# Score matmuls: the pass with the low queries on 64 of the 128 partitions, in pairs of row tiles

## The chip, the core and the metric

The program runs on one core of one Trainium2 chip. The metric is the device time of one execution in microseconds. Before the change the median of three runs is 1233.47 us (1231.24 to 1234.61).

Engines by their short names: PE (TensorE, matmuls), PEld (its weight loads), DVE (VectorE), ACT (ScalarE), POOL (GpSimd), SP (SyncE, which issues the DMAs).

## What is computed

One layer with three parts, all in float32:

```
x = x + cross_attention(layernorm(x), ctx, ctx)     # 8 batches, 64 queries, 1601 keys, 16 heads of 32
x = x + self_attention(layernorm(x)) @ Wo           # its value width is 0, so it adds nothing
x = x + moe(layernorm(x))                           # 8 experts, top 2, hidden 2048

# cross attention, the part that matters here
k = ctx @ Wk + bk ;  v = ctx @ Wv + bv              # ctx: 8 x 1601 x 384, Wk and Wv: 384 x 512
out = softmax(q @ k.T * 32**-0.5) @ v
```

## The kernel before

**Precision.** PE's single-pass float32 type (fp32r) keeps fewer bits than float32. So each operand is split into a high part (ACT or POOL rounds it) and a low part (what is left, by DVE or POOL), and a product is the sum of high times high, high times low and low times high (`three_pass`, L399).

**Attention.** The work is a sequence of 64 steps: 8 batches, and in each of them 8 steps s = 0 to 7. One step does two heads of one batch: the heads' 2 x 64 queries are the 128 columns of the weights (`qbd_hi`, `qbd_lo`; zero where a query meets the other head's rows), the two heads' 2 x 32 key dimensions are 64 rows. The 1601 keys lie in four chunks of 384, 384, 384 and 449 (computed as 450) keys; chunk c of a step has PSUM bank c for its scores.

`k_mix` holds for each step the high keys on one half of the 128 partitions and the low keys on the other half. Even steps have the high keys on partitions 0 to 63, odd steps on 64 to 127. A matmul with all 128 partitions so sums high and low keys in one pass. The queries stand on both halves. The scores of a chunk are two such matmuls: `qbd_hi` (L1321), and `qbd_lo` (L1322), which computes low queries times high keys, and low times low beside it.

**One step on PE** (`step`, L1311): the four chunks' scores; `context` of the step before (13 matmuls, L1285: probabilities times values); three units of the current projection job (`run_job`; a key unit is nine matmuls of 384 or 450 columns, a value unit nine of 256); 13 transposes of the probabilities (L1337), which write into the same four banks as the scores; the rest of the job's units. A job has five units, two of them keys, and every fourth job (that of steps 3 and 7) six. Step 0 has four small matmuls more (`spread`, L1293).

**One step on the others.** DVE takes the maximum of each chunk's scores (L955), the negated maximum of all (L958), takes up the context (L901, L911), splits off the low parts of the job's units (keys L877, values L884), then of the transposed probabilities chunk by chunk (`pt_mix`, L969), and then of the job's last two (or three) value units. ACT does the exponentials (L684, L687) after L958, then the high parts of the same units (keys L644, values L649) and of `pt_mix` (L695).

**What orders them.** Each engine runs its list in order, with semaphores between them. Three matter here: `pt_split` (DVE, one per chunk) says that a chunk's bank and the step's probabilities are read; the scores of chunk c of the next step wait for it (L1318). `scores_ready` (PE, one per chunk) releases DVE's maximum of that chunk (L954). `proj_split` gives a projection bank back.

**Setup.** The key weights are split once into `wk_hi` and `wk_lo` (L660, L859), [128, 3, 512] each. A key unit takes 128 columns of them as weights, so its PSUM rows 0 to 63 belong to the even step of a pair and rows 64 to 127 to the odd one. In the last batch the steps 4 to 7 have no projection job.

Of the kernel before, what the change touches and what calls it, by code (L numbers as in the profile page):

```python
# [25 lines left out]
ALU = mybir.AluOpType  # L26
ACT = mybir.ActivationFunctionType
# [11 lines left out]
def bass_perceiver_layer_kernel(nc, x, ctx_t, wq, bq_t, wk, bk_t, wv, bv_t, wo, bo, router_w, router_b,  # L39
# [54 lines left out]
    with ExitStack() as stack:  # L94
        def sb(name, shape, dt, where=stack):
            return where.enter_context(nc.sbuf_tensor(name, shape, dt))
# [10 lines left out]
        bq_sb = sb("bq_sb", [P, KD], F32)  # L107
        bk_sb = sb("bk_sb", [P, KD], F32)
        bv_sb = sb("bv_sb", [P, KD], F32)
# [55 lines left out]
        ctx_lo = [place(f"ctx_lo{i}", [P, KC, KEYS_PAD], F32R, attn) for i in range(2)]  # L165
        wk_hi = place("wk_hi", [P, KC, D], F32R, attn)
        wk_lo = place("wk_lo", [P, KC, D], F32R, attn)
        wv_hi = place("wv_hi", [P, KC, D], F32R, attn)
        wv_lo = place("wv_lo", [P, KC, D], F32R, attn)
        attn.close()  # L170

# [198 lines left out]
        def first_queries(quad, copy):  # L370
# [4 lines left out]
                    slice(NQ * (quad % 2), NQ * (quad % 2 + 1)))  # L375

        def x1_bank(t):

            return PROJ_BANK + t if t < TILES_BEFORE else t - TILES_BEFORE
# [29 lines left out]
        def _(sp):  # L409
# [16 lines left out]
            sp.dma_start(bq_sb[:], bq_t).then_inc(bias_loaded, 16)  # L426
            sp.dma_start(bk_sb[:], bk_t).then_inc(bias_loaded, 16)
            sp.dma_start(bv_sb[:], bv_t).then_inc(bias_loaded, 16)
# [191 lines left out]
        def _(act):  # L620
# [15 lines left out]
            def proj_high_part(unit, n, bank):  # L636

                kind, a, c = unit
                act.wait_ge(proj_ready, n + 1)
                if kind == "keys":  # L640
                    m = KEYS_EVEN[c]
                    for i in range(2):
                        rows = slice(i * HALF, (i + 1) * HALF)
                        last = nc.scalar.activation(k_mix[rows, 2 * a + i, KEY0[c]:KEY0[c] + m], ps[rows, bank, 0:m],  # L644
                                                    ACT.Identity, bias=bk_sb[rows, a:a + 1])
# [13 lines left out]
            act.wait_ge(wkv_loaded, 32)  # L659
            nc.scalar.copy(wk_hi[:], wkv_raw[:, 0]).then_inc(wkv_high, 1)  # L660
            nc.scalar.copy(wv_hi[:], wkv_raw[:, 1]).then_inc(wkv_high, 1)
            act.wait_ge(bias_loaded, 48)
            for c in range(CHUNKS):
# [156 lines left out]
        def _(dve):  # L820
# [36 lines left out]
            for i, (hi, lo) in enumerate([(wk_hi, wk_lo), (wv_hi, wv_lo)]):  # L857
                dve.wait_ge(wkv_high, i + 1)
                nc.vector.tensor_tensor(lo[:], wkv_raw[:, i], hi[:].bitcast(F32), ALU.subtract).then_inc(wkv_split, 1)  # L859
            dve.wait_ge(bias_loaded, 48)  # L860
            for m in range(KD):
# [7 lines left out]
            def proj_low_part(unit, n, bank):  # L869
                kind, a, c = unit  # L870
                dve.wait_ge(proj_high, n + 1)
                if kind == "keys":
                    m = KEYS_EVEN[c]
                    cols = slice(KEY0[c], KEY0[c] + m)
                    for i in range(2):
                        rows, other = slice(i * HALF, (i + 1) * HALF), slice((1 - i) * HALF, (2 - i) * HALF)
                        last = nc.vector.scalar_tensor_tensor(out=k_mix[other, 2 * a + i, cols], in0=ps[rows, bank, 0:m],  # L877
                                                              scalar=bk_sb[rows, a:a + 1],
                                                              in1=k_mix[rows, 2 * a + i, cols].bitcast(F32),
                                                              op0=ALU.add, op1=ALU.subtract)  # L880
# [342 lines left out]
        def _(pe):  # L1223
# [21 lines left out]
            def project(unit, n, bank):  # L1245
                kind, a, c = unit
                for k in range(KC):
                    if kind == "keys":
                        slot, m, cols = c % 2, KEYS_EVEN[c], slice(a * P, (a + 1) * P)
                        last = three_pass(pe, ps[:, bank, 0:m], wk_hi[:, k, cols], wk_lo[:, k, cols],  # L1250
                                          ctx_hi[slot][:, k, 0:m], ctx_lo[slot][:, k, 0:m], k == 0, k == KC - 1)
# [59 lines left out]
            def step(b, s, before, last_batch=False):  # L1311
# [4 lines left out]
                for c in range(CHUNKS):  # L1316
                    if before is not None:
                        pe.wait_ge(pt_split, CHUNKS * (n - 1) + c + 1)  # L1318
                    m = KEYS_EVEN[c]
                    cols = slice(KEY0[c], KEY0[c] + m)  # L1320
                    pe.matmul(ps[:, SCORE_BANK + c, 0:m], qbd_hi[:, s, :], k_mix[:, s, cols], start=True, stop=False)  # L1321
                    pe.matmul(ps[:, SCORE_BANK + c, 0:m], qbd_lo[:, s, :], k_mix[:, s, cols], start=False,  # L1322
                              stop=True).then_inc(scores_ready, 1)
                if before is not None:
# [228 lines left out]
```

## Time and profile before

| | us |
|---|---|
| median of 3 runs | 1233.47 |
| the profiled execution | 1227.9 |
| its span, first to last instruction | 1226.1 |
| PE busy | 1143.8 (93%) |
| DVE busy | 958.2 (78%) |
| ACT busy | 704.6 (57%) |
| POOL busy | 428.0 (35%) |

The attention steps fill some 60 to 790 us of the span; in 60 to 735 us PE is busy for 674.18 of 675.00 us at a granted clock of 1.00, DVE for 579.89 us. A busy PE means that some matmul is in flight: matmuls are pipelined, and how fast they follow one another is read from their starts, not from this share. The rest is the output projection, the router and the experts.

### The profile page before, as it was taken

How to read it: one execution, taken by the hardware profiler on the slowest of the kernel's cores; microseconds unless marked ns; L12 is line 12 of the kernel's file. 1: busy time of each engine (PE TensorE's matmuls, PEld its weight loads, DVE VectorE, ACT ScalarE, POOL GpSimd, SP SyncE). 2: the span in 40 equal slices, each digit the busy share in tenths (PEclk: the TensorE clock that was granted, in tenths of full speed). 3: DMA queues.
4: the chain of work that ended last, by engine and by line, in shares of the span. 5: the costliest groups of instructions: out<-in, count | busy, mean ns of one | idle time of the engine just before them, and what ended most of it. 6: DMA issues, size and time to landing. Idle time of an engine off the chain costs nothing.

```text
span 1226.1 us, 23151 instructions
## 1 busy us (share of the span) xinstructions
PE 1143.8 (93%) x7488; PEld 1054.2 (86%) x7489; DVE 958.2 (78%) x2082; ACT 704.6 (57%) x1418; POOL 428.0 (35%) x378
## 2 busy tenths in 40 slices
PE   4899999999999999999999998757889999889998
PEld 4799999999999999999999997635668898668897
DVE  6578888888888888888888888865876756876655
ACT  3456656656656656656656656443575565665654
POOL 5454754754654654654664640010000000000000
PEclk9899999999999999999999999966899999989999
DMA  5322122122122122122122103113755634655633
GB/s 181 101 63 62 40 70 61 38 70 61 38 70 61 38 70 61 38 70 61 39 69 61 58 23 118 50 52 105 244 189 184 206 109 164 221 191 193 201 117 103
DMA packets 74304, 121.15 MB, mean 99 GB/s; under 512 B 10776, under 2 KB 35480, under 8 KB 74272
## 3 DMA queue, kind: packets, MB, share of 16 engines
q1 hardware_dynamic: 74272, 120.73, 30.6%
q8 instruction: 19, 0.31, 0.1%
q14 instruction: 13, 0.11, 0.0%
HBM read 118.62 MB, written 2.10 MB: 98 GB/s over the span
## 4 chain that ended last, share of the span: by engine, by line
PE 79%; DVE 9%; ACT 5%; DMA 3%; issue 3%; DVEq 0%; SPq 0%; ACTq 0%
PE ps L401 18%; PE ps L403 17%; PE ps L402 17%; PE ps L1285 7%; PE ps L1337 7%; PE ps L1321 4%; PE ps L1322 3%; DMA w_raw<-in_w_dram 2%; PE ps L1386 2%; DVE w_lo L1027 2%; DVE mx L955 1%; DVE k_mix L877 1%; PE ps L1429 1%; DVE w_lo L1019 1%; PE ps L1430 1%
## 5 line engine op out<-in xcount | busy, mean ns | idle before, releaser
L545 POOL TENSOR_TENSOR ctx_hi<-ctx_raw,no_query 128x1152 fp32r<-128x1152 f32 x64 | 142.8, 2231 | 290.2 <-PE ps L403 281.2
L877 DVE SCALAR_TENSOR_TENSOR k_mix<-ps,bk_sb,k_mix 64x384 fp32r<-64x384 f32 (+1 forms) x256 | 162.3, 634 | 82.1 <-ACT k_mix L644 77.8
L684 ACT ACTIVATE probs<-ps,negmax 128x1152 f32<-128x1152 f32 x64 | 78.3, 1223 | 201.1 <-DVE negmax L958 201.1
L401 PE MATMUL ps<-wv_hi,ctx_hi 128*128 128x256 f32 (+1 forms) x624 | 181.8, 291 | 6.7 <-DVE k_mix L877 6.5
L549 POOL TENSOR_TENSOR ctx_lo<-ctx_raw,ctx_hi 128x1152 fp32r<-128x1152 f32 x64 | 179.7, 2808 | 5.0
L403 PE MATMUL ps<-wv_hi,ctx_lo 128*128 128x256 f32 (+1 forms) x624 | 175.7, 282 | 0.0
L402 PE MATMUL ps<-wv_lo,ctx_hi 128*128 128x256 f32 (+1 forms) x624 | 174.9, 280 | 0.0
L644 ACT ACTIVATE k_mix<-ps,bk_sb 64x384 fp32r<-64x384 f32 (+1 forms) x256 | 150.8, 589 | 24.0 <-PE ps L403 19.4
L969 DVE TENSOR_TENSOR pt_mix<-ps,pt_mix 128x384 fp32r<-128x384 f32 (+1 forms) x256 | 142.2, 580 | 1.4 <-ACT pt_mix L695 1.4
L401 PE MATMUL ps<-ctx_hi,wk_hi 128*128 128x384 f32 (+1 forms) x384 | 133.2, 347 | 0.0
L403 PE MATMUL ps<-ctx_hi,wk_lo 128*128 128x384 f32 (+1 forms) x384 | 132.3, 345 | 0.0
L402 PE MATMUL ps<-ctx_lo,wk_hi 128*128 128x384 f32 (+1 forms) x384 | 131.9, 344 | 0.0
L955 DVE TENSOR_REDUCE mx<-ps 128x1 f32<-128x384 f32 (+1 forms) x256 | 128.6, 564 | 0.6 <-issue 0.2
L649 ACT CAST v_mix<-ps 128x256 fp32r<-128x256 f32 (+1 forms) x208 | 77.5, 373 | 85.3 <-PE ps L403 83.4
L401 PEld LDWEIGHTS ps<-wv_hi,ctx_hi 128*128 128x128 f32 (+1 forms) x624 | 115.8, 186 | 9.1 <-DVE k_mix L877 8.1
L402 PEld LDWEIGHTS ps<-wv_lo,ctx_hi 128*128 128x128 f32 (+1 forms) x624 | 116.3, 186 | 0.3
L403 PEld LDWEIGHTS ps<-wv_hi,ctx_lo 128*128 128x128 f32 (+1 forms) x624 | 115.7, 185 | 0.0
L695 ACT CAST pt_mix<-ps 128x384 fp32r<-128x384 f32 (+1 forms) x256 | 111.5, 532 | 0.1
L1285 PEld LDWEIGHTS ps<-pt_mix,v_mix 128*128 128x128 f32 (+1 forms) x832 | 106.2, 188 | 2.1
L1285 PE MATMUL ps<-pt_mix,v_mix 128*128 128x256 f32 (+1 forms) x832 | 107.6, 279 | 0.0
L1337 PE MATMUL ps<-ident,probs 128*128 128x128 f32 (+1 forms) x832 | 101.4, 273 | 6.5 <-ACT probs L684 6.5
L401 PE MATMUL ps<-w_hi,h_hi 128*128 128x512 f32 x192 | 81.3, 423 | 19.6 <-DVE h_lo L1205 19.5
(219 smaller groups left out, 2668.5 us busy)
## 6 DMA issues: line engine op xcount, KB each, us to landing
w_raw<-in_w_dram SPq DMA_DIRECT2D x68, 1024.0 KB, 5.3
ctx_raw<-in_ctx_t_dram SPq DMA_DIRECT2D x48, 576.0 KB, 3.8
ctx_raw<-in_ctx_t_dram SPq DMA_DIRECT2D x16, 673.5 KB, 4.1
q_both<-q_scratch SPq DMA_DIRECT2D x14, 128.0 KB, 3.1
x<-in_x_dram SPq DMA_DIRECT2D x1, 1024.0 KB, 5.4
wq_raw<-in_wq_dram SPq DMA_DIRECT2D x1, 1024.0 KB, 7.7
q_scratch<-q_out SPq DMA_DIRECT2D x1, 1024.0 KB, 5.4
wo_raw<-in_wo_dram SPq DMA_DIRECT2D x1, 1024.0 KB, 5.4
```

The costliest lines, as they stand in the source:

```text
L401: pe.matmul(acc_ap, a_hi, b_hi, start=start, stop=False)
L402: pe.matmul(acc_ap, a_hi, b_lo, start=False, stop=False)
L403: return pe.matmul(acc_ap, a_lo, b_hi, start=False, stop=stop)
L545: nc.gpsimd.tensor_tensor(ctx_hi[slot][:, :, 0:n], ctx_raw[slot][:, :, 0:n], no_query[:].rearrange("p (o i) -> p o i", o=1).broadcast_to([ ...
L549: nc.gpsimd.tensor_tensor(ctx_lo[slot][:, :, 0:n], ctx_raw[slot][:, :, 0:n], ctx_hi[slot][:, :, 0:n].bitcast(F32), ALU.subtract).then_inc( ...
L644: last = nc.scalar.activation(k_mix[rows, 2 * a + i, KEY0[c]:KEY0[c] + m], ps[rows, bank, 0:m], ACT.Identity, bias=bk_sb[rows, a:a + 1])
L695: nc.scalar.copy(pt_mix[:, TILE0[c]:TILE0[c] + n, 0, :], ps[:, SCORE_BANK + c, 0:n * P].rearrange("p (t r) -> p t r", t=n)).then_inc(pt_hi ...
L877: last = nc.vector.scalar_tensor_tensor(out=k_mix[other, 2 * a + i, cols], in0=ps[rows, bank, 0:m], scalar=bk_sb[rows, a:a + 1], in1=k_mix ...
L955: part = nc.vector.tensor_reduce(mx[:, c:c + 1], ps[:, SCORE_BANK + c, 0:KEYS[c]], AX.X, ALU.max)
L969: nc.vector.tensor_tensor(pt_mix[:, TILE0[c]:TILE0[c] + m, 1, :], ps[:, SCORE_BANK + c, 0:m * P].rearrange("p (t r) -> p t r", t=m), pt_mi ...
L1285: last = pe.matmul(ps[:, PV_BANK, 0:2 * P], v_mix[0:r, t, s, :, :], pt_mix[0:r, t, :, :], start=(t == 0), stop=(t == KT - 1))
L1337: last = pe.transpose(ps[0:r, SCORE_BANK + c, i * P:(i + 1) * P], probs[:, key:key + r], ident[:])
```

## The change

The pass with `qbd_lo` takes only the 64 partitions that hold the high keys. For two chunks in a row to lie on different halves, the half with the high keys now also changes with the chunk: partitions 64 * ((s + c) % 2) and the 63 behind it. So the matmuls of chunks 0, 1, 2, 3 lie alternately in one and the other half of PE's rows. For this the projection of the odd chunks must give its two halves swapped: `wk_hi` and `wk_lo` become [128, 3, 4, 192], with the first 64 columns of each group once more at its end, an odd chunk takes columns 64 to 191, and there is a second, swapped key bias. The step issues the four `qbd_hi` matmuls first, then the four `qbd_lo` ones.

```
-                    pe.matmul(ps[:, SCORE_BANK + c, 0:m], qbd_hi[:, s, :], k_mix[:, s, cols], start=True, stop=False)
-                    pe.matmul(ps[:, SCORE_BANK + c, 0:m], qbd_lo[:, s, :], k_mix[:, s, cols], start=False,
-                              stop=True).then_inc(scores_ready, 1)
+                    pe.matmul(ps[:, SCORE_BANK + c, 0:m], qbd_hi[:, s, :], k_mix[:, s, KEY0[c]:KEY0[c] + m],
+                              start=True, stop=False)
+                for c in range(CHUNKS):
+                    m, rows = KEYS_EVEN[c], high_half(s, c)
+                    pe.matmul(ps[:, SCORE_BANK + c, 0:m], qbd_lo[rows, s, :], k_mix[rows, s, KEY0[c]:KEY0[c] + m],
+                              start=False, stop=True).then_inc(scores_ready, 1)
...
+        def high_half(s, c):
+            return slice((s + c) % 2 * HALF, ((s + c) % 2 + 1) * HALF)
...
-                        slot, m, cols = c % 2, KEYS_EVEN[c], slice(a * P, (a + 1) * P)
+                        slot, m, cols = c % 2, KEYS_EVEN[c], slice(c % 2 * HALF, c % 2 * HALF + P)
...
-            nc.scalar.copy(wk_hi[:], wkv_raw[:, 0]).then_inc(wkv_high, 1)
+            for cols, to in key_columns():
+                last = nc.scalar.copy(wk_hi[:, :, :, to], wkv_raw[:, 0].rearrange("p k (g c) -> p k g c", c=P)[:, :, :, cols])
+            last.then_inc(wkv_high, 1)
...
-            sp.dma_start(bk_sb[:], bk_t).then_inc(bias_loaded, 16)
+            sp.dma_start(bk_sb[0][:], bk_t).then_inc(bias_loaded, 16)
+            for i in range(2):
+                sp.dma_start(bk_sb[1][i * HALF:(i + 1) * HALF], bk_t[(1 - i) * HALF:(2 - i) * HALF]).then_inc(bias_loaded, 16)
```

On ACT and DVE the splits of the keys take the rows by `high_half` and the bias by the chunk's parity; their number and shapes stay. DVE's `wk_lo` is made in two pieces like `wk_hi`.

PE's list at the scores of a step and the start of the context behind them, before (k_mix are the keys, qbd_hi and qbd_lo the queries):

```order
L1321 MATMUL ps<-k_mix,qbd_hi 128x384 [waits pt_split]
L1322 MATMUL ps<-k_mix,qbd_lo 128x384
L1318 REGISTER_ALU
L1321 MATMUL ps<-k_mix,qbd_hi 128x450 [waits pt_split]
L1322 MATMUL ps<-k_mix,qbd_lo 128x450
L1280 ISA
L1281 ISA [waits proj_split]
L1282 ISA [waits pt_split]
L1285 MATMUL ps<-pt_mix,v_mix 128x256 [waits pv_free]
```

(The first three rows stand there three times.) The same place in the changed kernel:

```order
L1339 MATMUL ps<-k_mix,qbd_hi 128x384 [waits pt_split]
L1337 REGISTER_ALU
L1339 MATMUL ps<-k_mix,qbd_hi 128x450 [waits pt_split]
L1343 MATMUL ps<-k_mix,qbd_lo 128x384 x3
L1343 MATMUL ps<-k_mix,qbd_lo 128x450
L1299 ISA
L1300 ISA [waits proj_split]
L1301 ISA [waits pt_split]
L1304 MATMUL ps<-pt_mix,v_mix 128x256 [waits pv_free]
```

All four qbd_lo matmuls, and with them the first of the four releases of DVE's maxima, have moved behind the last of the four waits for `pt_split`.

DVE's list in the setup, before, from the split of the key weights to the first query tile:

```order
L855 TENSOR_TENSOR xt_lo<-ps,xt_hi 128x512 [waits xt_high] x4
L859 TENSOR_TENSOR wk_lo<-wkv_raw,wk_hi 128x1536 [waits wkv_high]
L859 TENSOR_TENSOR wv_lo<-wkv_raw,wv_hi 128x1536 [waits wkv_high]
L863 TENSOR_SCALAR q_out<-ps,bq_sb 128x512 [waits q_ready,bias_loaded]
L863 TENSOR_SCALAR q_out<-ps,bq_sb 128x512 [waits q_ready] x3
```

And in the changed kernel:

```order
L870 TENSOR_TENSOR xt_lo<-ps,xt_hi 128x512 [waits xt_high] x4
L874 TENSOR_TENSOR wk_lo<-wkv_raw,wk_hi 128x12x128 [waits wkv_high]
L874 TENSOR_TENSOR wk_lo<-wkv_raw,wk_hi 128x12x64
L878 TENSOR_TENSOR wv_lo<-wkv_raw,wv_hi 128x1536 [waits wkv_high]
L882 TENSOR_SCALAR q_out<-ps,bq_sb 128x512 [waits q_ready,bias_loaded]
L882 TENSOR_SCALAR q_out<-ps,bq_sb 128x512 [waits q_ready] x3
```

One piece of 12 x 64 elements has come in ahead of the value weights.

## Rows read from the trace of the kernel before

**Rows 1.** The page: busy time by engine; the chain that ended last, by engine.

```profile
PE 1143.8 (93%) x7488; PEld 1054.2 (86%) x7489; DVE 958.2 (78%) x2082; ACT 704.6 (57%) x1418; POOL 428.0 (35%) x378
...
PE 79%; DVE 9%; ACT 5%; DMA 3%; issue 3%; DVEq 0%; SPq 0%; ACTq 0%
```

**Rows 2.** Waits: engine, line waited for; us in total, times, longest.

```profile
DVE k_mix L877 <- ACT k_mix L644: 77.8, 73, 3.1
...
PEld ps L1321 <- DVE pt_mix L969: 12.6, 49, 0.3
```

**Rows 3.** Timeline of PE, step 6's scores: start, us, instruction, count.

```profile
317.60 0.47 PE L1321 MATMUL ps<-k_mix,qbd_hi 128*128 128x450 f32 x1
317.91 0.37 PE L1322 MATMUL ps<-k_mix,qbd_lo 128*128 128x450 f32 x1
318.11 1.64 PE L1285 MATMUL ps<-pt_mix,v_mix 128*128 128x256 f32 x13
```

**Rows 4.** Timeline of DVE, steps 5 and 6; in brackets idle time and releaser.

```profile
307.07 2.01 DVE L955 TENSOR_REDUCE mx<-ps 128x1 f32<-128x384 f32 x4
...
312.32 2.53 DVE L877 SCALAR_TENSOR_TENSOR k_mix<-ps,bk_sb,k_mix 64x384 fp32r<-64x384 f32 x4 [1.20 <-ACT k_mix L644]
...
316.39 1.15 DVE L969 TENSOR_TENSOR pt_mix<-ps,pt_mix 128x384 fp32r<-128x384 f32 x2
...
318.12 2.01 DVE L955 TENSOR_REDUCE mx<-ps 128x1 f32<-128x384 f32 x4
```

**Rows 5.** Timeline of PE, steps 0 and 1, first scores and first context.

```profile
340.08 0.34 PE L1321 MATMUL ps<-k_mix,qbd_hi 128*128 128x384 f32 x1
340.26 0.34 PE L1322 MATMUL ps<-k_mix,qbd_lo 128*128 128x384 f32 x1
...
341.55 1.69 PE L1285 MATMUL ps<-pt_mix,v_mix 128*128 128x256 f32 x13
...
352.43 0.34 PE L1321 MATMUL ps<-k_mix,qbd_hi 128*128 128x384 f32 x1
```

**Rows 6.** Timeline of DVE, steps 0 and 1, and step 0 a batch later.

```profile
341.02 2.00 DVE L955 TENSOR_REDUCE mx<-ps 128x1 f32<-128x384 f32 x4
...
353.04 0.42 DVE L884 TENSOR_TENSOR v_mix<-ps,v_mix 128x256 fp32r<-128x256 f32 x1 [0.39 <-ACT v_mix L649]
353.55 2.02 DVE L955 TENSOR_REDUCE mx<-ps 128x1 f32<-128x384 f32 x4
...
432.57 2.00 DVE L955 TENSOR_REDUCE mx<-ps 128x1 f32<-128x384 f32 x4
```

**Rows 7.** Timeline of PE, transposes and L1297's 16-row tiles, then L401.

```profile
303.17 0.60 PE L1337 MATMUL ps<-ident,probs 128*128 128x128 f32 x4
303.52 0.36 PE L401 MATMUL ps<-wv_hi,ctx_hi 128*128 128x256 f32 x1
303.72 0.28 PE L402 MATMUL ps<-wv_lo,ctx_hi 128*128 128x256 f32 x1
...
349.19 1.10 PE L1297 MATMUL ps<-rinv_t,pick 16*128 16x64 f32 x8
350.22 0.39 PE L401 MATMUL ps<-wv_hi,ctx_hi 128*128 128x256 f32 x1
350.44 0.28 PE L402 MATMUL ps<-wv_lo,ctx_hi 128*128 128x256 f32 x1
```

**Rows 8.** L1297's matmuls, by line: ns min/median/max, first and last start, forms.

```profile
L1297 PE MATMUL ps<-rinv_t,pick x64: 270/270/319, 166.0 to 794.3; 16*128 16x64 f32 x64
```

**Rows 9.** Timeline of DVE in the setup.

```profile
19.43 3.09 DVE L859 TENSOR_TENSOR wk_lo<-wkv_raw,wk_hi 128x1536 fp32r<-128x1536 f32 x1 [0.57 <-ACT wk_hi L660]
...
26.03 2.20 DVE L863 TENSOR_SCALAR q_out<-ps,bq_sb 128x512 f32<-128x512 f32 x3
30.19 0.75 DVE L863 TENSOR_SCALAR q_out<-ps,bq_sb 128x512 f32<-128x512 f32 x1 [1.97 <-PE ps L403]
```

**Rows 10.** Timeline of ACT, step 7 of the last batch.

```profile
784.68 1.22 ACT L684 ACTIVATE probs<-ps,negmax 128x1152 f32<-128x1152 f32 x1 [6.11 <-DVE negmax L958]
```

More of the change, by code:

```diff
@@ L107, in bass_perceiver_layer_kernel @@
         bq_sb = sb("bq_sb", [P, KD], F32)
-        bk_sb = sb("bk_sb", [P, KD], F32)
+        bk_sb = [sb(f"bk_sb{i}", [P, KD], F32) for i in range(2)]
         bv_sb = sb("bv_sb", [P, KD], F32)
@@ L165, in bass_perceiver_layer_kernel @@
         ctx_lo = [place(f"ctx_lo{i}", [P, KC, KEYS_PAD], F32R, attn) for i in range(2)]
-        wk_hi = place("wk_hi", [P, KC, D], F32R, attn)
-        wk_lo = place("wk_lo", [P, KC, D], F32R, attn)
         wv_hi = place("wv_hi", [P, KC, D], F32R, attn)
         wv_lo = place("wv_lo", [P, KC, D], F32R, attn)
+        wk_hi = place("wk_hi", [P, KC, GROUPS, P + HALF], F32R, attn)
+        wk_lo = place("wk_lo", [P, KC, GROUPS, P + HALF], F32R, attn)
         attn.close()
@@ L375, in first_queries, with key_columns @@
                     slice(NQ * (quad % 2), NQ * (quad % 2 + 1)))
+        def key_columns():
+            return [(slice(0, P), slice(0, P)), (slice(0, HALF), slice(P, P + HALF))]
+        def high_half(s, c):
+            return slice((s + c) % 2 * HALF, ((s + c) % 2 + 1) * HALF)
         def x1_bank(t):
@@ L642, in proj_high_part @@
                     for i in range(2):
-                        rows = slice(i * HALF, (i + 1) * HALF)
+                        rows = high_half(2 * a + i, c)
                         last = nc.scalar.activation(k_mix[rows, 2 * a + i, KEY0[c]:KEY0[c] + m], ps[rows, bank, 0:m],
-                                                    ACT.Identity, bias=bk_sb[rows, a:a + 1])
+                                                    ACT.Identity, bias=bk_sb[c % 2][rows, a:a + 1])
                     last.then_inc(proj_high, 1)
@@ L659, in _ @@
             act.wait_ge(wkv_loaded, 32)
-            nc.scalar.copy(wk_hi[:], wkv_raw[:, 0]).then_inc(wkv_high, 1)
+            for cols, to in key_columns():
+                last = nc.scalar.copy(wk_hi[:, :, :, to], wkv_raw[:, 0].rearrange("p k (g c) -> p k g c", c=P)[:, :, :, cols])
+            last.then_inc(wkv_high, 1)
             nc.scalar.copy(wv_hi[:], wkv_raw[:, 1]).then_inc(wkv_high, 1)
-            act.wait_ge(bias_loaded, 48)
+            act.wait_ge(bias_loaded, 80)
             for c in range(CHUNKS):
@@ L856, in _ @@
                                         ALU.subtract).then_inc(xt_split, 1)
[L857 to L860, printed above, removed]
+            dve.wait_ge(wkv_high, 1)
+            for cols, to in key_columns():
+                last = nc.vector.tensor_tensor(wk_lo[:, :, :, to], wkv_raw[:, 0].rearrange("p k (g c) -> p k g c", c=P)[:, :, :, cols],
+                                               wk_hi[:, :, :, to].bitcast(F32), ALU.subtract)
+            last.then_inc(wkv_split, 1)
+            dve.wait_ge(wkv_high, 2)
+            nc.vector.tensor_tensor(wv_lo[:], wkv_raw[:, 1], wv_hi[:].bitcast(F32), ALU.subtract).then_inc(wkv_split, 1)
+            dve.wait_ge(bias_loaded, 80)
             for m in range(KD):
@@ L875, in proj_low_part @@
                     for i in range(2):
-                        rows, other = slice(i * HALF, (i + 1) * HALF), slice((1 - i) * HALF, (2 - i) * HALF)
+                        rows, other = high_half(2 * a + i, c), high_half(2 * a + i + 1, c)
                         last = nc.vector.scalar_tensor_tensor(out=k_mix[other, 2 * a + i, cols], in0=ps[rows, bank, 0:m],
-                                                              scalar=bk_sb[rows, a:a + 1],
+                                                              scalar=bk_sb[c % 2][rows, a:a + 1],
                                                               in1=k_mix[rows, 2 * a + i, cols].bitcast(F32),
@@ L1248, in project @@
                     if kind == "keys":
-                        slot, m, cols = c % 2, KEYS_EVEN[c], slice(a * P, (a + 1) * P)
-                        last = three_pass(pe, ps[:, bank, 0:m], wk_hi[:, k, cols], wk_lo[:, k, cols],
+                        slot, m, cols = c % 2, KEYS_EVEN[c], slice(c % 2 * HALF, c % 2 * HALF + P)
+                        last = three_pass(pe, ps[:, bank, 0:m], wk_hi[:, k, a, cols], wk_lo[:, k, a, cols],
                                           ctx_hi[slot][:, k, 0:m], ctx_lo[slot][:, k, 0:m], k == 0, k == KC - 1)
@@ L1319, in step @@
                     m = KEYS_EVEN[c]
-                    cols = slice(KEY0[c], KEY0[c] + m)
-                    pe.matmul(ps[:, SCORE_BANK + c, 0:m], qbd_hi[:, s, :], k_mix[:, s, cols], start=True, stop=False)
-                    pe.matmul(ps[:, SCORE_BANK + c, 0:m], qbd_lo[:, s, :], k_mix[:, s, cols], start=False,
-                              stop=True).then_inc(scores_ready, 1)
+                    pe.matmul(ps[:, SCORE_BANK + c, 0:m], qbd_hi[:, s, :], k_mix[:, s, KEY0[c]:KEY0[c] + m],
[4 more added lines that the diff above has]
+                              start=False, stop=True).then_inc(scores_ready, 1)
                 if before is not None:
```

## The prediction

> **What bounds the kernel now.** The page comes first: PE is busy for 93% of the span and holds 79% of the chain that ended last [rows 1]. Read alone, that says that whatever PE saves is saved. The view of waits speaks against it: in the steps DVE waits 77.8 us, all of it for ACT's high keys, and PE's weight loads for the scores wait 12.6 us in 49 places, 0.3 us at most, for DVE's split of the probabilities [rows 2]. So the timelines of one step have to be laid side by side.
>
> In an ordinary step DVE starts its maxima at 307.07 and, one step later, at 318.12: 11.05 us [rows 4]. Between the two it waits only once, 1.20 us for ACT's keys, which stand behind the exponentials, which stand behind the maxima. This is a loop of DVE and ACT that PE isn't in: first maximum, exponentials, keys, low keys, low probabilities, next first maximum. Call T the end of the last split of the probabilities, 316.39 + 1.15 = 317.54 [rows 4]. PE's qbd_hi matmul of chunk 3 starts at 317.60, 0.06 behind T: PE waited for DVE, and its context starts at 318.11, T + 0.57 [rows 3]. DVE's first maximum starts at 318.12, T + 0.58 [rows 4], behind the job's last two value splits, with chunk 0's scores long there.
>
> Behind the job with six units it is different. PE starts the scores of step 0 at 340.08 [rows 5], and DVE's maximum starts at 341.02, 0.94 later [rows 6]. At step 1 PE starts at 352.43 [rows 5], DVE waited 0.39 for the last value unit, which comes from PE by way of ACT, and starts its maximum at 353.55, 1.12 later [rows 6]. There PE is late. So the path through a batch (91.55 us, 341.02 to 432.57 [rows 6]) is mixed: DVE and ACT from step 1's maximum to T of step 3; PE from there through the six units to step 4; DVE and ACT again to T of step 7; PE through steps 7 and 0 to step 1. Steps 4 to 7 repeat the pattern of 0 to 3.
>
> **What is removed.** Four matmuls of 128 rows per step become four of 64 rows. One 384-column matmul follows the next by 0.18 us (340.08, 340.26), the whole scores pass takes 341.55 - 340.08 = 1.47 us [rows 5], half of it, 0.73, the low pass. In perfect pairs it would take 0.37.
>
> **What is added on PE: changes of the tile.** The scores now go from 128-row tiles to 64-row tiles and back. The trace has no 64-row tile; the nearest rows are L1297's matmuls on a 16-row tile. Leaving them: the last of the eight starts at 349.19 + 1.10 - 0.27 = 350.02 [rows 7, 8], the second matmul behind it (L402) at 350.44, 0.42 later. At transposes of the full tile the same stretch is 303.17 + 0.60 - 0.27 = 303.50 to 303.72, 0.22, with the same 0.27 taken for a transpose [rows 7]. So a change costs about 0.20 us: the next matmul starts only as the last one is nearly through (0.07 before its end), and its weights aren't loaded ahead. I take 0.21, since here the matmuls are longer; two per step. The lower bound is 0 (the 64-row tile may not empty the array), the upper one 0.42 for each. The Trainium skill has the rule in "TensorEngine Tiling (Array Packing)", Key Properties: changing the tiling mode, not just the tile, drains the engine. The trace agrees with it for 16 rows.
>
> **Whether the pairs run together** no row shows. The matmuls still need four weight loads; the transposes, whose 128 columns are as many as their weights', follow each other by (0.60 - 0.27)/3 = 0.11 us [rows 7, 8], so I take 0.11 from one low matmul to the next, the last one 0.33 behind the first. Bounds: 0.18 behind it (two perfect pairs), or 0.53 (one after the other). The Trainium skill, "TensorE: Matmul & The Clock Gate", Part 3, gives starts some 4 ns apart for matmuls on different rows; by it the 0.18 would hold, and the sum below would be the smaller one named there.
>
> **What is moved.** All four low matmuls now stand behind the wait of qbd_hi's chunk 3 for T. Before, two matmuls followed T; now five do, and the first chunk's scores are ready only after two of them. Counted from T: qbd_hi of chunk 3 starts at 0.06; the next matmul follows it by 0.31 after such a wait (317.60 to 317.91 [rows 3]), and by 0.21 more for the tile: 0.58. It takes 0.34 [rows 5], and a semaphore 0.06 (what T to 317.60 took): DVE's first maximum can start at 0.98, where it started at 0.58. The context follows the last low matmul (0.58 + 0.33 = 0.91) by 0.20 as before (317.91 to 318.11 [rows 3]) and 0.21: 1.32, where it was 0.57. In steps where PE is the late one, counted from the scores' start: the low pass begins at 4 matmuls + 0.21 = 0.73 + 0.21 = 0.94, the first maximum at 0.94 + 0.40 = 1.34, the context at 0.94 + 0.33 + 0.41 = 1.68.
>
> **The sum of one batch,** along its path:
> - steps 2, 5, 6: first maximum 0.98 for 0.58 behind T, 3 x 0.40 = 1.20
> - steps 3 and 7: context 1.32 for 0.57 behind T, 2 x 0.75 = 1.50
> - step 0: scores pass 1.68 for 1.47, 0.21
> - step 4: first maximum 1.34 for 0.94 behind the scores' start, 0.40
> - step 1: 1.34 for 1.12, 0.22
>
> Together 3.53 us. 60 of the 64 steps, 7.5 batches, are like this: 26.5 us. With perfect pairs 3 x 0.15 less per batch (both contexts and step 0): 3.08, 23 us. With no overlap at all 3 x 0.20 more: 4.13, 31 us.
>
> **At nothing.** The last batch's steps 5 to 7 have no job; there ACT waits up to 6.11 us for the maximum, which stands behind other work of DVE [rows 10], and the scores are ready long before; if that cover were gone, 4 x 0.4 = 1.6 us. Setup: wk_lo grows by half, 1.5 us by its 3.09 [rows 9], and ACT's wk_hi by less. DVE's query tiles would start at 27.6 for 26.03 and end at 29.8, and the last of them waits for PE until 30.19 anyway, after 1.97 us of idling [rows 9]. Three bias DMAs for one delay what SP issues behind them by about a microsecond, which the same 30 us of query projection cover. If neither were covered, it would be some 1.5 us. Swapped halves of keys on ACT and DVE are as many and as large as before: 0.
>
> The profiled execution took 1227.9 with a span of 1226.1; with 26.5 it is 1254.4. The median of the runs lies 5.6 above it (1233.47), so the median after: 1260.
>
> **The rivals.**
> (a) The tile change costs nothing, or little, for a 64-row tile. For it: only 16 rows were seen. Against: the gaps are the same on entering that tile and leaving it. Then counted from T the first maximum is at 0.77 (+0.19) and the context at 0.90 (+0.33); PE's pass is 1.47 - 0.20; step 4 +0.19, step 1 +0.01. Per batch 0.57 + 0.66 - 0.20 + 0.20 = 1.23: 9 us, 1243; with perfect pairs 0.78: 6 us, 1239. Still slower, by the order alone.
> (b) PE is what bounds every step, and pairs run together: 64 x (0.73 - 0.37) = 23 us less, 1210. For it: PE's 93% and the chain's 79% [rows 1]. Against: DVE's step of 11.05 us, in which no wait is for PE, and the 49 waits of PE for DVE [rows 2, 4]. It decides if the first maximum isn't held back, that is if chunk 0's scores arrive by T + 0.58; but they come from a matmul behind qbd_hi of chunk 3, which alone lasts until T + 0.53 (317.60 + 0.47 [rows 3]).
> (c) A change from one 64-row tile to the other empties the array too. Then the low pass is 3 x 0.41 long for 0.33, 0.9 us more at three places of the batch: 2.7, 20 us on top, 1280. Nothing in the trace speaks for it but that it wasn't seen.
> (d) All of it is absorbed somewhere: 1233. Against: DVE's loop has no idle time but the wait for ACT that is itself behind the maximum.
>
> **How the numbers follow.** The forecast (1255 to 1266, its own range) 68%, (a) 13%, (b) 7%, (c) 7%, (d) 5%. Range: from (a)'s 1240 over the forecast to 1269 for what an upper tile cost would add. 0.3%, about 3.7 us, is what a measurement can tell from no change. Faster: (b), 0.07, and a little of (a) and (d): 0.08. Same: (d) and the rest of (a)'s edge, 0.06. Slower 0.86.
>
> **What would show it.** In the changed trace: DVE's first maximum some 0.98 behind the end of the last pt_mix split, with an idle time before it put down to PE's qbd_lo matmul; waits before qbd_hi's chunk 3 in most steps, longer than 0.3 us; 0.2 more than before between the last qbd_hi and the first qbd_lo, and between the last qbd_lo and the second context matmul; low matmuls 0.11 apart; a batch of about 95.1 us for 91.55. Wrong it would be if the low matmuls of two chunks start together right behind qbd_hi and DVE's maxima still start without a wait.

## The result and the profile after

The changed kernel takes 1255.04 us (median of 4 runs, 1254.57 to 1255.71), the kernel before beside it 1232.36 (4 runs, 1229.85 to 1234.61): 1.0197 times as long, with an interval from 1.0179 to 1.0216. By the ratio it is 24 us slower, by the medians 22.7; 1260 was forecast. The profiled execution has a span of 1253.1 us for 1226.1, 27.0 more.

The page of the changed kernel, busy time and the chain that ended last, as in [rows 1]:

```profile
PE 1162.9 (93%) x7488; PEld 1031.3 (82%) x7489; DVE 955.2 (76%) x2083; ACT 704.4 (56%) x1419; POOL 426.5 (34%) x378
...
PE 51%; DVE 25%; issue 11%; ACT 9%; DMA 3%; DVEq 1%; SPq 0%; ACTq 0%
```

PE's share is what it was, though half of its low work is gone, and its part of the chain has fallen from 79% to 51%, DVE's has grown. The chain switched over to DVE while the kernel became slower: its shares told little of what a cheaper PE pass would be worth.

Its waits (engine, line waited for; us in total, times, longest), as in [rows 2]:

```profile
DVE k_mix L896 <- ACT k_mix L657: 92.8, 73, 3.1
...
PEld ps L1339 <- DVE pt_mix L988: 32.2, 88, 0.4
...
PEld ps L1304 <- issue: 17.6, 63, 0.3
...
DVE mx L974 <- PE ps L1343: 16.6, 61, 0.3
...
PEld ps L1343 <- issue: 15.2, 64, 0.3
```

Three of these lines are new. DVE's maxima wait for the low matmuls in 61 of 64 steps, 0.27 each; the weight loads behind either change of the tile start late (L1343 and L1304, "issue": 0.24 and 0.28 each). And PE waits for the splits of the probabilities in 88 places where it was 49.

An ordinary step, PE and its weight loads, as in [rows 3]:

```profile
327.67 1.09 PE L1339 MATMUL ps<-k_mix,qbd_hi 128*128 128x384 f32 x3
328.92 0.47 PE L1339 MATMUL ps<-k_mix,qbd_hi 128*128 128x450 f32 x1 [0.16 <-DVE pt_mix L988]
329.32 0.64 PE L1343 MATMUL ps<-k_mix,qbd_lo 64*128 64x384 f32 x4
329.89 1.80 PE L1304 MATMUL ps<-pt_mix,v_mix 128*128 128x256 f32 x13
```

```profile
329.32 0.30 PEld L1343 LDWEIGHTS ps<-k_mix,qbd_lo 64*128 64x128 f32 x4 [0.21 <-issue]
```

And DVE in the same step, as in [rows 4], and in step 0 of two batches, as in [rows 6]:

```profile
327.72 1.15 DVE L988 TENSOR_TENSOR pt_mix<-ps,pt_mix 128x384 fp32r<-128x384 f32 x2
328.78 0.74 DVE L903 TENSOR_TENSOR v_mix<-ps,v_mix 128x256 fp32r<-128x256 f32 x2
329.79 2.02 DVE L974 TENSOR_REDUCE mx<-ps 128x1 f32<-128x384 f32 x4 [0.27 <-PE ps L1343]
...
353.64 2.02 DVE L974 TENSOR_REDUCE mx<-ps 128x1 f32<-128x384 f32 x4 [0.28 <-PE ps L1343]
...
448.29 2.02 DVE L974 TENSOR_REDUCE mx<-ps 128x1 f32<-128x384 f32 x4 [0.28 <-PE ps L1343]
```

T is 327.72 + 1.15 = 328.87. PE's last qbd_hi matmul starts 0.05 behind it, the first low one at T + 0.45, DVE's maximum at T + 0.92 (it was T + 0.58), the context at T + 1.02 (it was T + 0.57). From the last qbd_hi to the context it was 0.51 (317.60 to 318.11 [rows 3]) and is now 0.97 (328.92 to 329.89).

The batch takes 448.29 - 353.64 = 94.65 us there, 94.61 as the mean over seven batches, where the same mean of the kernel before is 91.56. From the first maximum of the kernel to that of step 60 (7.5 batches) the trace has 709.2 us for 686.0, 23.2 more; the first maximum comes 3.0 later (70.7 for 67.7), and what follows step 60 lasts 0.8 longer. 23.2 + 3.0 + 0.8 = 27.0, the difference of the spans. It is more than the 22.7 of the medians because the profiled execution of the kernel before is a short one, 4.5 us under its median; that of the changed kernel lies at its median.

### The profile page after: what moved, and what is told of

Read it like the earlier page. It is cut to its first block, busy times and chain, and to the rows that moved or that the text cites. A ratio compares the mean times of both kernels' runs of the same rounds, so it can differ in the third digit from the quotient of the medians.

```text
span 1253.1 us, 23155 instructions
## 1 busy us (share of the span) xinstructions
PE 1162.9 (93%) x7488; PEld 1031.3 (82%) x7489; DVE 955.2 (76%) x2083; ACT 704.4 (56%) x1419; POOL 426.5 (34%) x378
## 4 chain that ended last, share of the span: by engine, by line
PE 51%; DVE 25%; issue 11%; ACT 9%; DMA 3%; DVEq 1%; SPq 0%; ACTq 0%
PE ps L412 12%; PE ps L413 11%; PE ps L414 11%; DVE mx L974 6%; DVE k_mix L896 5%; DVE pt_mix L988 5%; ACT k_mix L657 4%; PE ps L1304 3%; PE ps L1339 3%; PE ps L1358 3%; DMA w_raw<-in_w_dram 2%; PE ps L1343 2%; PE ps L1407 2%; DVE w_lo L1046 2%; ACT probs L699 1%
## 5 line engine op out<-in xcount | busy, mean ns | idle before, releaser
L1304 PEld LDWEIGHTS ps<-pt_mix,v_mix 128*128 128x128 f32 (+1 forms) x832 | 101.8, 188 | 17.7 <-issue 17.6
L1304 PE MATMUL ps<-pt_mix,v_mix 128*128 128x256 f32 (+1 forms) x832 | 114.9, 288 | 0.0
```

The costliest lines, as they stand in the source:

```text
L1304: last = pe.matmul(ps[:, PV_BANK, 0:2 * P], v_mix[0:r, t, s, :, :], pt_mix[0:r, t, :, :], start=(t == 0), stop=(t == KT - 1))
```

## The experiments

Each was timed against runs of the kernel before on the same chip. T and "first maximum" are as in the prediction; "batch" is the mean of seven batches of a profiled execution (first maximum of step 4 to that of step 60), 91.56 us in the kernel before, "scores pass" the time from the first qbd_hi matmul to the first context matmul of a step.

### The order alone, on 128 rows

From the kernel before: the four low matmuls behind the four qbd_hi ones, still full tiles.

```diff
                     pe.matmul(ps[:, SCORE_BANK + c, 0:m], qbd_hi[:, s, :], k_mix[:, s, cols], start=True, stop=False)
+                for c in range(CHUNKS):
+                    m = KEYS_EVEN[c]
+                    cols = slice(KEY0[c], KEY0[c] + m)
                     pe.matmul(ps[:, SCORE_BANK + c, 0:m], qbd_lo[:, s, :], k_mix[:, s, cols], start=False,
```

> The kernel before with one edit: the step issues its four qbd_hi matmuls first and then its four qbd_lo matmuls, all with 128 rows as before. Theory (the order holds the chain back, the change of tile costs PE time): only the order's part appears. The first maximum can start 0.06 + 0.31 + 0.34 + 0.06 = 0.77 us behind the last pt_mix split for 0.58, the context starts at 1.1 for 0.57, step 4 loses 0.19; per batch 0.57 + 1.06 + 0.20 = 1.8 us, 14 us in all: 1246 against 1232.4. DVE waits for qbd_lo before its first maximum, by about 0.1 us. Rival (the order costs nothing, all of the loss is the array emptying between tile sizes): within 2 us of the kernel before, 1232.

Measured: 1245.33 us, 1.0125 (1.0107 to 1.0142), batch 93.24, 1.7 more. PE, then DVE in an ordinary step:

```profile
322.12 0.47 PE L1321 MATMUL ps<-k_mix,qbd_hi 128*128 128x450 f32 x1 [0.16 <-DVE pt_mix L969]
322.43 0.90 PE L1325 MATMUL ps<-k_mix,qbd_lo 128*128 128x384 f32 x4
323.16 1.69 PE L1285 MATMUL ps<-pt_mix,v_mix 128*128 128x256 f32 x13
```

```profile
320.92 1.15 DVE L969 TENSOR_TENSOR pt_mix<-ps,pt_mix 128x384 fp32r<-128x384 f32 x2
321.98 0.75 DVE L884 TENSOR_TENSOR v_mix<-ps,v_mix 128x256 fp32r<-128x256 f32 x2
322.81 2.02 DVE L955 TENSOR_REDUCE mx<-ps 128x1 f32<-128x384 f32 x4
```

T is 322.07; the first maximum starts at T + 0.74 for 0.58, the context at T + 1.09 for 0.57. The PE work is that of before to the instruction. So some 15 of the 24 us are the order alone: all four low matmuls stand behind the wait for T.

### The layout alone

From the changed kernel: the low pass back on 128 rows and each chunk's behind its high one. The swapped halves, the larger weight tiles and the biases stay.

```diff
-                              start=True, stop=False)
-                for c in range(CHUNKS):
-                    m, rows = KEYS_EVEN[c], high_half(s, c)
-                    pe.matmul(ps[:, SCORE_BANK + c, 0:m], qbd_lo[rows, s, :], k_mix[rows, s, KEY0[c]:KEY0[c] + m],
-                              start=False, stop=True).then_inc(scores_ready, 1)
+                    pe.matmul(ps[:, SCORE_BANK + c, 0:m], qbd_lo[:, s, :], k_mix[:, s, cols], start=False,
+                              stop=True).then_inc(scores_ready, 1)
```

> The changed kernel with the step of the kernel before: the key weights with 192 columns per group, the swapped halves of k_mix and the extra bias loads stay, but the scores are issued chunk by chunk with 128 rows. Theory: these edits are hidden, within 2 us of the kernel before. Rival: the 2 to 3 us that the profile of the changed kernel is longer in its setup come from the larger key weights and the bias loads, 1235.

Measured: 1233.69 us, 1.0025 (1.0015 to 1.0035); batch 91.83. About 3 us, small but not nothing. From step 1 to 2 and from 5 to 6, where the job's keys are those of an odd chunk, the first maxima are 11.20 apart for 11.06, 2 of the 3 us in all, and the timeline of ACT shows where. This kernel first, then the kernel before:

```profile
360.67 0.20 ACT L702 ACTIVATION_READ_ACCUMULATOR probs<-ps,negmax 128x1 f32 x1
360.89 2.36 ACT L657 ACTIVATE k_mix<-ps,bk_sb 64x384 fp32r<-64x384 f32 x4
```

```profile
357.52 0.20 ACT L687 ACTIVATION_READ_ACCUMULATOR probs<-ps,negmax 128x1 f32 x1
357.61 2.35 ACT L644 ACTIVATE k_mix<-ps,bk_sb 64x384 fp32r<-64x384 f32 x4
```

The first instruction on the keys starts 0.22 behind the start of the accumulator's read (the instruction behind each exponential that takes its row sums) for 0.09. With the layout the first half taken for an odd chunk is the upper one, partitions 64 to 127. Whether that is it, the next experiment asks.

### The lower half first

From the last one: for odd chunks ACT and DVE take the halves in the other order. The same instructions, in pairs swapped.

```diff
-                    for i in range(2):
+                    for i in ((1, 0) if c % 2 else (0, 1)):
                         rows = high_half(2 * a + i, c)
...
-                    for i in range(2):
+                    for i in ((1, 0) if c % 2 else (0, 1)):
                         rows, other = high_half(2 * a + i, c), high_half(2 * a + i + 1, c)
```

> The kernel of e2_layout_only (1233.7, a batch of 91.9 us for 91.55) with one edit: for the odd chunks ACT and DVE take the key unit's lower 64 partitions first and the upper ones second, as they do for even chunks. In e2's trace the steps with an odd chunk's job are 0.13 us longer, and ACT's first key piece starts 0.22 us behind the start of the exponentials' last accumulator read for 0.09. Theory: it is the order of the halves; with it turned the batch is 91.6 us again and 1 to 2 us are won, 1232. Rival (it is the swapped halves as such, or chance): a batch of 91.9, 1234.

Measured: 1229.45 us, 0.999 (0.9977 to 1.0002, 12 runs), batch 91.59. ACT:

```profile
359.96 0.20 ACT L702 ACTIVATION_READ_ACCUMULATOR probs<-ps,negmax 128x1 f32 x1
360.05 2.36 ACT L657 ACTIVATE k_mix<-ps,bk_sb 64x384 fp32r<-64x384 f32 x4
```

0.09 again, the batch and the time are those of before. The cost that the layout had in the steps was the order of the halves. The edit turns it on DVE as well, but the start that moved is ACT's.

### No pairs: all high keys of a step on one half

From the changed kernel: `high_half` no longer depends on the chunk, so all four low matmuls of a step are on the same 64 rows.

```diff
-            return slice((s + c) % 2 * HALF, ((s + c) % 2 + 1) * HALF)
+            return slice(s % 2 * HALF, (s % 2 + 1) * HALF)
...
-                        slot, m, cols = c % 2, KEYS_EVEN[c], slice(c % 2 * HALF, c % 2 * HALF + P)
+                        slot, m, cols = c % 2, KEYS_EVEN[c], slice(0, P)
```

Both biases become `bk_sb[0]`.

> The changed kernel, but the high keys lie on one half for all four chunks of a step (the half alternates with the step, as before), so that the four 64-row matmuls are on the same row tile and can't run beside one another. Theory: pairs run together in the changed kernel (the trace shows four in 0.28 us); here they follow one another by 0.18 us, so that the context and the last chunk's scores come 0.25 to 0.35 us later: 3 x 0.3 = 0.9 us per batch, 7 us slower than the changed kernel, 1262. Rival (the starts of the pairs in the trace are a model and they don't run together): the same as the changed kernel, 1255.

Measured: 1264.75 us, 1.0278 (1.0262 to 1.0293), batch 95.84, 1.2 more than with pairs. (The lower half is also first again here, which gives back the 0.13 at two steps, so that the pairs themselves are worth some 1.5 per batch.) PE, then its weight loads:

```profile
320.07 1.00 PE L1343 MATMUL ps<-k_mix,qbd_lo 64*128 64x384 f32 x4
321.00 1.80 PE L1304 MATMUL ps<-pt_mix,v_mix 128*128 128x256 f32 x13
```

```profile
320.07 0.65 PEld L1343 LDWEIGHTS ps<-k_mix,qbd_lo 64*128 64x128 f32 x4 [0.21 <-issue]
```

Four low matmuls take 1.00 us for 0.64, their weight loads 0.65 for 0.30, and from the first of them to the context it is 0.93 for 0.57 (329.32 to 329.89 above). 0.36 is the whole saving that the change was built on: the pairs do run together. By their single starts in the changed kernel the two of a pair begin 3 ns apart in the median, 12 at most, and the second pair 0.28 us behind the first. This kernel also goes to 64 rows and back once a step, so the cost of those two changes is in both.

### A low matmul behind each high one

From the changed kernel: its low matmuls stay on 64 rows, but each stands behind its own chunk's qbd_hi. Eight changes of the tile per step for two.

```diff
                               start=True, stop=False)
-                for c in range(CHUNKS):
-                    m, rows = KEYS_EVEN[c], high_half(s, c)
                     pe.matmul(ps[:, SCORE_BANK + c, 0:m], qbd_lo[rows, s, :], k_mix[rows, s, KEY0[c]:KEY0[c] + m],
```

> The changed kernel, but each chunk's 64-row qbd_lo matmul follows its qbd_hi matmul at once, so that the tile changes eight times per step instead of twice. Theory (0.2 us for each change of tile size on PE, either way): the scores pass takes 1.47 + 8 x 0.2 = 3.1 us, PE becomes the bound of every step, a batch takes 79 + 8 x 3.1 = 104 us for 91.6, and the whole is 90 us slower, 1320. Rival (a change is free, what costs is the order): the order is that of the kernel before, so 1232.

Measured: 1317.94 us (2 runs), 1.071 (1.0688 to 1.0732), batch 103.18. PE, one scores pass:

```profile
324.60 0.34 PE L1340 MATMUL ps<-k_mix,qbd_hi 128*128 128x384 f32 x1
324.87 0.43 PE L1342 MATMUL ps<-k_mix,qbd_lo 64*128 64x384 f32 x1
325.23 0.44 PE L1340 MATMUL ps<-k_mix,qbd_hi 128*128 128x384 f32 x1
325.60 0.44 PE L1342 MATMUL ps<-k_mix,qbd_lo 64*128 64x384 f32 x1
...
327.51 1.75 PE L1304 MATMUL ps<-pt_mix,v_mix 128*128 128x256 f32 x13
```

The pass is 2.91 long for 1.47 [rows 5]: 1.44 for eight changes, 0.18 each. In its middle the starts are 0.36 to 0.37 apart for 0.18 without a change: 0.19, into the 64-row tile and out of it alike. The very first is 0.27 behind: 0.09 of a change shows ahead of the first matmul on the new tile, the rest behind it. The changed kernel has the same. Its first low matmul is 0.40 behind the last qbd_hi (328.92, 329.32) for 0.31 with the same order on 128 rows (322.12, 322.43), and the second context matmul is 0.23 behind the first for 0.12.

### No low pass at all

From the kernel before, the four low matmuls left out.

> The kernel before without the four qbd_lo matmuls of each step (the low parts of the queries are left out of the scores). It shows what the low pass is worth if it costs nothing at all: PE has 0.73 us less to do in every step. Theory (most steps are bound by the loop of DVE and ACT): a batch gets down to what that loop allows, 91.55 less the 0.39 at step 1, some 0.06 at steps 0 and 4 and 0.08 at step 5, about 91.0; 4 to 5 us faster, 1228. Rival (PE is the bound): 64 x 0.73 = 47 us faster, 1185.

Measured: 1230.05 us, 0.9998 (0.9986 to 1.0011, 12 runs). Removing twice what the change could save gives nothing. But in the profiled execution two amounts stand against each other. The batch is 1.1 shorter (90.48), 7.6 us up to step 60; what follows step 60 lasts 5.5 longer. Its timeline of PE, in the experts' part that none of this touches:

```profile
971.81 0.40 PE L1429 MATMUL ps<-y_lo,sel_t 128*128 128x512 f32 x1
975.65 0.38 PE L401 MATMUL ps<-xg_hi,w_hi 128*128 128x256 f32 x1 [3.44 <-issue]
```

PE stands still for 3.44 us with nothing that the profile shows to wait for. Its clock behind that, by the table of windows (stretch, its length, busy time and count of PE, PEld, DVE, ACT and POOL, granted clock, DMA share, GB/s):

```profile
972.00:976.00 4.00, 0.56 (x4) 0.36 (x4) 1.15 (x4) 0.00 (x0) 0.00 (x0) 1.00 0.03 11
976.00:982.00 6.00, 6.00 (x37) 5.82 (x36) 0.43 (x1) 2.17 (x6) 0.00 (x0) 0.72 0.00 0
982.00:990.00 8.00, 8.00 (x54) 7.31 (x53) 4.15 (x6) 4.87 (x9) 0.00 (x0) 1.00 0.00 0
```

0.72 is a mean over both levels, 1.2 and 2.4 GHz, and by an estimate costs another 6 x 0.28 = 1.7: 5.1 of the 5.5. Of the thirteen kernels traced three have such a gap between 930 and 1200: this one, the other one without a low pass (3.3) and the one with eight changes (6.0); in the rest it is 0.2 at most. The view of the DMA queues in this kernel from 974.6 to 975.6 has one packet, and it is one of instructions:

```profile
q8 instruction: 1, 0.02, 5.5%
```

In the trace it runs from 974.64 to 975.52, and PE goes on at 975.65. In the other kernel without a low pass such a packet ends at 965.22 where PE goes on at 965.18; in the one with eight changes it ends 1.7 ahead. That fits a PE that waits for its instructions, but no run tests it, and what sets the gap off stays open. If the gap is in the timed runs as well (one execution was profiled), this kernel would without it be some 5 us faster than before, still far from the 64 x 0.73 = 47 us of PE work removed.

### The last chunk apart

From the changed kernel: the low matmuls of chunks 0 to 2 on 64 rows ahead of the wait for T, chunk 3 whole on 128 rows behind it.

```diff
+                for c in range(FULL):
...
+                    scores(c)
+                for c in range(FULL):
+                    scores(c, high_half(s, c), low=True)
+                if before is not None:
+                    pe.wait_ge(pt_split, CHUNKS * n)
+                scores(FULL)
+                scores(FULL, low=True)
```

> The changed kernel with another order of the step: qbd_hi of chunks 0 to 2, then their 64-row qbd_lo (chunks 0 and 1 as a pair), and only then the wait for the last pt_mix split and chunk 3 with both matmuls on 128 rows. The tile changes twice as in the changed kernel, but nothing but chunk 3's two matmuls stands behind the last wait. Theory: the first maximum and the context are again where they were, 0.58 behind the last split; left are 0.2 us of PE time at step 0 and 0.2 at step 4, 0.4 per batch: 3 us slower than the kernel before, 1236. Rival (the tiles cost, not the order): as slow as the changed kernel, 1255.

Measured: 1240.88 us, 1.008 (1.0067 to 1.0093), batch 92.95. I had 1236. Fourteen us of the change's cost go when only two matmuls follow T again, but not all. PE, one pass:

```profile
332.72 0.80 PE L1337 MATMUL ps<-k_mix,qbd_hi 128*128 128x384 f32 x3
333.45 0.62 PE L1337 MATMUL ps<-k_mix,qbd_lo 64*128 64x384 f32 x3
334.00 0.47 PE L1337 MATMUL ps<-k_mix,qbd_hi 128*128 128x450 f32 x1
334.31 0.37 PE L1337 MATMUL ps<-k_mix,qbd_lo 128*128 128x450 f32 x1
334.51 1.70 PE L1304 MATMUL ps<-pt_mix,v_mix 128*128 128x256 f32 x13
```

One pair saves 0.18 and two changes cost 0.38: where PE is late the pass is 1.68 long for 1.47 (1.79 here, with a wait for the split of chunk 2 in it). It makes PE late at T too: the last qbd_hi starts at T + 0.38 and the context of steps 3 and 7 at T + 0.89 for 0.57, twice 0.32 per batch where I had nothing. I had taken PE to have more slack than that. The 0.13 of ACT at two steps comes on top.

### The maxima first

From the kernel before, an edit on DVE alone: the value splits that stood between the last probability split and the next step's maxima now stand behind the maxima.

```diff
                 if before is not None:
+                    if not (last and before[1] >= CHUNKS):
+                        job_low(*before, range(EARLY, UNITS[before[1] % CHUNKS]))
                     take_context(*before)
...
-                if has_job:
-                    job_low(b, s, range(EARLY, UNITS[s % CHUNKS]))
```

> The kernel before with one edit on DVE: the low parts of a job's last value units are split off behind the maxima of the next step, not ahead of them. DVE then does them while it would wait for ACT's keys, and its loop gets shorter by up to 0.66 us per step. Theory: the loop is no longer the bound, PE is, whose work is about 90.6 us per batch for 91.55; 7 us faster, 1225. Rival (the projection banks come free too late and PE waits for them, or the context comes too late): no gain or slower, 1232 to 1240.

Measured: 1226.15 us, 0.9961 (0.9948 to 0.9974), batch 90.95. It beats both kernels. DVE:

```profile
314.60 1.15 DVE L971 TENSOR_TENSOR pt_mix<-ps,pt_mix 128x384 fp32r<-128x384 f32 x2
315.66 2.01 DVE L955 TENSOR_REDUCE mx<-ps 128x1 f32<-128x384 f32 x4
317.70 0.16 DVE L958 TENSOR_REDUCE negmax<-mx 128x1 f32<-128x4 f32 x1
317.80 0.75 DVE L884 TENSOR_TENSOR v_mix<-ps,v_mix 128x256 fp32r<-128x256 f32 x2
```

The maximum starts at T - 0.09 for T + 0.58, since chunk 0's scores are there. The step up to it took 10.65 us for 11.05 (from 305.01), and PE no longer waits for T: its last qbd_hi starts at T + 0.27 to 0.34.

### The same edit on the changed kernel

> The changed kernel with the same edit on DVE as the run before. Theory: with DVE off the path its maxima start when the scores are there, and what the change costs is then PE's own time: a scores pass of 1.47 - 0.35 + 0.42, hardly more than before, and what PE still waits for behind the last split. 3 to 10 us slower than the same edit without the tiles, 1228 to 1235. Rival (the tile changes alone make the 23 us): 23 us slower than it, 1248.

Measured: 1264.79 us, 1.0275 (1.0262 to 1.0288), batch 95.93: ten us slower than the change without it, where I had thought it would win all back. DVE:

```profile
329.63 1.14 DVE L990 TENSOR_TENSOR pt_mix<-ps,pt_mix 128x384 fp32r<-128x384 f32 x2
331.70 2.02 DVE L974 TENSOR_REDUCE mx<-ps 128x1 f32<-128x384 f32 x4 [0.93 <-PE ps L1343]
...
333.85 0.76 DVE L903 TENSOR_TENSOR v_mix<-ps,v_mix 128x256 fp32r<-128x256 f32 x2
```

T is 330.77, and the maximum starts at T + 0.93, as before the edit. I had forgotten that PE's low pass is itself behind T: in the changed kernel DVE's splits, PE's last high and first low matmul, and DVE's maximum form one loop. The value splits only filled its 0.6 us; moved away, they leave DVE idle, so nothing is won. The ten us lost have another cause. They fall on steps 0 and 4 alone (from there to the next first maximum 13.00 for 12.42 and 12.15 for 11.41), behind the jobs with six units. There PE now waits for a value split that stands behind the maxima, since it gives a projection bank back; the waits of this kernel have a line that the changed kernel's do not:

```profile
PE ps L412 <- DVE v_mix L903: 8.7, 14, 0.7
```

### The edit and the last chunk apart

> The kernel of e6_last_apart (64-row pair for chunks 0 and 1, chunk 3 whole and last, two changes of tile) with DVE's edit of e7_max_first. Theory: the chain from the last split to the first maximum is short here (e8_max_first_tiles had all four low matmuls behind it and lost 38 us to e7), so PE is the bound, and the two changes less the one pair cost 0.21 us in every step, not only at two: 8 x 0.21 = 1.7 us per batch, 13 us slower than e7, 1239. Rival (with DVE relaxed the tile changes are hidden): as e7, 1226.

Measured: 1243.26 us, 1.0108 (1.0092 to 1.0125), batch 93.35, 17 us more than the DVE edit alone. I had 1239. The same two matmuls follow T in both. The main part is PE's own balance, a pass of 1.68 for 1.47, 8 x 0.21 = 1.7 of the 2.4 per batch; PE also waits 14 times for a projection bank as in the last run, 3.5 us in all, and the rest isn't taken apart. Once DVE's loop is short, the tiles are a plain loss.

### The edit without the low pass

> The kernel of e7_max_first (1226.2, a batch of 90.9 us) without the four qbd_lo matmuls of each step (the low parts of the queries are left out of the scores). Theory: with DVE's loop shortened by 0.66 us PE is the bound, and PE's saving now counts until that loop binds again at 11.05 - 0.66 = 10.4 us for an ordinary step that takes 10.7: some 0.3 us per step or more, 86 to 88.5 us per batch, 18 to 35 us faster than e7, about 1200. Rival (the low pass is worth nothing here either): as e5_no_low against the kernel before, within 3 us of e7.

Measured: 1215.93 us, 0.9887 (0.9868 to 0.9905), batch 88.74, 2.2 less than with the low pass; 16.1 us from the first maximum to step 60 in the trace, of which a start 1.6 later and an end 6.3 longer (the gap of PE again) take 7.9 back. I had 1200; less than half of that gain came. PE waits for T again (its last qbd_hi at T + 0.06 in ordinary steps), and for a projection bank in 14 places, 6.5 us. Removing the low pass was worth nothing to the kernel before and 10 us here, in the attention alone 7.6 and 16.1. So PE's work counts for more where DVE's loop covers less of it.

## Why the prediction was right

**What bounds the kernel** was read rightly: in ordinary steps DVE's loop with ACT, and PE in the steps behind the big job. Rival (b), which went by the page's 93% and 79% [rows 1], had 1210; leaving the low pass out altogether gave 1230.05, nothing. One reading was a little off: from 60 to 735 us DVE waits 71.0 us for ACT's high keys, but also 4.4 for its values and 1.9 for PE, so not all of its waiting is for the keys.

**What is moved** was right, and is most of the cost: 1.7 of 3.05 us per batch with the order alone. First maximum T + 0.98 forecast, T + 0.92 measured.

**The tile change** was right in size: 0.21 forecast from a 16-row tile [rows 7, 8], 0.18 to 0.19 measured with eight of them per step. It was put wholly ahead of the first matmul on the new tile, though, and only 0.09 stands there. So the first low matmul starts at T + 0.45 and not 0.58; from there to the maximum it is 0.47 for 0.40, which makes T + 0.92 and not 0.98. Rival (a), free changes, is out, and so is (c): a change from one 64-row half to the other empties nothing, since then the pairs' low pass would be longer than the 0.57 that it takes.

**Whether the pairs run together** was the mis-sized term: 0.11 from one low matmul to the next was taken; perfect pairs it is. The prediction's sum for them was 3.08 us per batch, the trace has 94.61 - 91.56 = 3.05. The Trainium skill, "TensorE: Matmul & The Clock Gate", Part 3, gives matmuls on different rows starts some 4 ns apart. The trace agrees: 3 ns in the median within a pair, the four weight loads take 0.30 us together, and the low pass up to the context 0.57, where 0.93 stood without pairs.

That the two sums agree to 0.03 is partly luck. Along the path the trace has, as means over six batches: the first maximum 0.35 later behind T at steps 2, 5 and 6 (0.40 forecast); the context 0.46 later at steps 3 and 7 with 0.11 more behind its first matmul (0.60 with perfect pairs); the pass of step 0 0.07 shorter, with the same 0.11 (0.06 longer); 0.37 at step 4 (0.40) and 0.17 at step 1 (0.22). Together that is 2.8, 0.3 under the sum, and the 0.13 of ACT at two steps, which had been put at nothing, fills the rest. The 0.11 was guessed from transposes [rows 7, 8] that all use one full tile; it says nothing of two tiles side by side.

**At nothing** held for the last batch and failed twice, for small amounts. ACT pays 0.13 at steps 1 and 5 for beginning with the upper half. And the setup isn't free. DVE there, as in [rows 9]:

```profile
20.54 4.74 DVE L874 TENSOR_TENSOR wk_lo<-wkv_raw,wk_hi 128x1536 fp32r<-128x1536 f32 x2 [1.42 <-ACT wk_hi L674]
25.21 4.23 DVE L878 TENSOR_TENSOR wv_lo<-wkv_raw,wv_hi 128x1536 fp32r<-128x1536 f32 x1
29.36 2.06 DVE L882 TENSOR_SCALAR q_out<-ps,bq_sb 128x512 f32<-128x512 f32 x3
32.41 0.75 DVE L882 TENSOR_SCALAR q_out<-ps,bq_sb 128x512 f32<-128x512 f32 x1 [0.99 <-PE ps L414]
```

The query tiles start at 29.36 for 26.03, not 27.6: wk_lo takes 4.74 (3.09 and half of it, 4.6, was forecast), but ACT's wk_hi makes it wait 1.42 for 0.57 [rows 9], so that it starts 1.1 later, and wv_lo takes 4.23 for 3.66. The last one comes at 32.41 for 30.19, here also because PE's query matmuls ran at the lower clock for longer (0.43 apart until 23.25, 0.23 after). In four of eight traces with this layout that was so, in the others the query tiles were late by DVE alone; the first maximum came at 69.1 to 70.7 in all eight, and at 67.6 to 68.0 in four of five with the old layout (69.6 in the fifth, with slow query matmuls too). The timed runs of the lower-half kernel, which has this setup, show no loss (0.999), so how much of it a usual execution pays stays open.

**The level**: the forecast is 5 us too high. 26.5 us were put on the median, where the medians lie 22.7 apart, the 3.53 x 7.5 of the sum being 3.05 x 7.5 = 23 in the trace; and the median of before came out 1.1 lower (1232.36 for 1233.47). The range's upper end, 1269, is less than its own reason gives: with the upper bound of 0.42 per change the sum grows by 11 x 0.21 = 2.3 per batch, which is 1277.

## What to carry over

Before cheapening work on a busy engine, cut it out altogether and time that: here it gave nothing, and the first such experiment would have told it. Count what stands between the last input that arrives and the first output that is waited for; batching like operations behind one wait moves all of them behind the latest input. A pair of 64-row matmuls of 384 columns saves 0.18 us and a change of the tile costs 0.19 each way, so the two pairs of a step (0.36) do not quite pay for going there and back (0.38), and one pair is far from it.

## What was not expected of the hardware

- Two fp32r matmuls on different halves of the rows and 384 columns run together, and so do their weight loads (four in 0.30 us); but the load behind a change of the tile isn't done ahead (0.24 and 0.28 of idle time, "issue"). Of a change's 0.19 only 0.09 stands ahead of the first matmul, the rest behind it.
- An ACT instruction behind the read of an accumulator started 0.13 later when it was on partitions 64 to 127 than on 0 to 63 (0.22 for 0.09). With the halves in that order the kernel took 1.0025 times as long as before, with the other order 0.999.
- In three of thirteen kernels PE stood still once for 3.3 to 6.0 us, far behind the edited code and with nothing to wait for but, perhaps, its own instructions, and in the two without a low pass what follows step 60 was 5.5 and 6.3 us longer. Such kernels are best compared by stretches of the trace, not by their ends alone.
